# A two-layer vision tower on one core: weights centred before x lands, means accumulated beside, and one-hot products, first sums and gate products reordered

## What is computed

```
h = patches @ Wp + bp + (relu(xy @ W1 + b1) @ W2 + b2)      # embedding and position
h = h + attn0(LN(h))        # 8 query heads of 64, one shared key and value
h = h + ffn0(LN(h))         # gelu MLP, only for the tokens whose weight ranks in the top 31 of an image
h = h + attn1(LN(h))        # bias per key from the LAST edge that points at it, out of 16384 edges
h = h + moe(LN(h))          # top 2 of 8 experts
```

## Time and profile before

| what | value |
|---|---|
| median of three timed runs | 71.36 us |
| the profiled execution, its own time | 71.47 us |
| its span, first to last instruction | 69.6 us |
| PE matmul busy | 60.6 us, 87% of the span |
| DVE / ACT / POOL busy | 41.7 / 29.7 / 13.5 us |
| share of the chain that ended last | PE 61%, DVE 12%, DMA 9%, ACT 7%, POOL 3% |

### The profile page before, as it was taken

One profiled execution on the slowest core, in us unless ns is written; L12 is line 12 of the kernel. 1 busy time (PEld: TensorE's weight loads), 2 busy tenths in 40 slices (PEclk: granted clock), 3 DMA queues, 4 the chain that ended last, 5 costly groups with the idle time before them and its releaser, 6 DMA issues.

```text
span 69.6 us, 1990 instructions
## 1 busy us (share of the span) xinstructions
PE 60.6 (87%) x830; PEld 39.6 (57%) x839; DVE 41.7 (60%) x111; ACT 29.7 (43%) x69; POOL 13.5 (19%) x32
## 2 busy tenths in 40 slices
PE   3995896999999999999989995959999969989940
PEld 1330462787698578564448565548794318654910
DVE  2491039975699995535962546999563025756830
ACT  0240012431748852177764425259604283953030
POOL 6800039200000892058304000000000004000000
PEclk9999999999999999999999999999999999999999
DMA  0799999950000000000000000000000000000003
GB/s 0 182 381 370 392 225 243 235 175 0 0 9 0 0 0 9 0 0 5 0 0 0 0 9 5 0 9 0 0 9 0 0 0 0 0 0 0 0 0 75
DMA packets 2390, 4.07 MB, mean 58 GB/s; under 512 B 780, under 2 KB 1230, under 8 KB 2382
## 3 DMA queue, kind: packets, MB, share of 16 engines
q1 hardware_dynamic: 1568, 3.49, 17.4%
q10 hardware_dynamic: 781, 0.46, 2.2%
q0 software_dynamic: 32, 0.00, 0.0%
HBM read 3.82 MB, written 0.13 MB: 57 GB/s over the span
## 4 chain that ended last, share of the span: by engine, by line
PE 61%; DVE 12%; DMA 9%; ACT 7%; POOL 3%; issue 3%; DVEq 0%; ACTq 0%; POOLq 0%
DMA Xt<-in_x_dram 9%; PE psum L717 8%; PE psum L711 6%; DVE top L533 4%; ACT ge L457 3%; POOL WoS L300 3%; PE psum L727 3%; PE psum L928 3%; PE psum L974 3%; PE psum L819 3%; PE psum L770 3%; PE psum L1066 2%; PE psum L746 2%; DVE E L632 2%; DVE top L630 2%
## 5 line engine op out<-in xcount | busy, mean ns | idle before, releaser
L717 PE MATMUL psum<-warm 128*128 128x512 bf16 x44 | 14.5, 441 | 1.7 <-DVE warm L479 1.2
L717 PEld LDWEIGHTS psum<-warm 128*128 128x128 bf16 x53 | 5.2, 109 | 6.8 <-issue 3.6
L300 POOL TENSOR_TENSOR WoS<-pack_attn,top 128x256 f32<-128x256 f32 x5 | 3.1, 647 | 10.1 <-DVE top L540 10.1
L492 DVE TENSOR_TENSOR onehot<-idb,iota 128x2048 bf16<-128x2048 bf16 x4 | 4.8, 1241 | 0.0
L335 POOL TENSOR_TENSOR resT<-hT,xC 128x256 f32<-128x256 f32 x1 | 0.7, 724 | 20.0 <-DVE xC L661 20.0
L428 ACT ACTIVATE E<-E 128x512 f32<-128x512 f32 x4 | 2.5, 631 | 3.1 <-DVE E L632 3.1
L727 PE MATMUL psum<-Xt,pack_wp 128*64 128x256 f32 x16 | 2.2, 390 | 1.1 <-DMA Xt<-in_x_dram 1.1
L457 ACT ACTIVATE ge<-psum,pack_moe 128x512 f32<-128x512 f32 x4 | 2.5, 687 | 1.2 <-PE psum L1026 1.2
L711 PE MATMUL psum<-pack_ident,E 128*128 128x128 f32 x16 | 2.5, 276 | 0.7 <-DVE E L632 0.7
L630 DVE TENSOR_REDUCE top<-psum 128x8 f32<-128x512 f32 x4 | 2.7, 683 | 0.4 <-PE psum L943 0.4
L498 DVE TENSOR_TENSOR centre<-pack_ident,mean 128x128 f32<-128x128 f32 x1 | 0.3, 293 | 4.4 <-DMA pack_ident<-in_ident_dram 4.4
(11 more groups left out here) (206 smaller groups left out, 134.6 us busy)
## 6 DMA issues: line engine op xcount, KB each, us to landing
Xt<-in_x_dram SPq DMA_DIRECT2D x1, 1024.0 KB, 6.4
Xt<-in_x_dram SPq DMA_DIRECT2D x1, 512.0 KB, 7.4
pack_both<-in_both_dram SPq DMA_DIRECT2D x2, 240.2 KB, 8.8
pack_moe<-in_moe_dram SPq DMA_DIRECT2D x1, 450.0 KB, 9.8
pack_mid<-in_mid_dram SPq DMA_DIRECT2D x1, 327.5 KB, 9.7
pack_attn<-in_attn_dram SPq DMA_DIRECT2D x1, 288.0 KB, 8.0
pack_expert<-in_expert_dram SPq DMA_DIRECT2D x2, 130.0 KB, 9.4
pack_wp<-in_wp_dram ACTq DMA_DIRECT2D x1, 192.0 KB, 5.8
```

The lines of the kernel that those rows point to most:

```text
L300: gp.tensor_tensor(WoS[:, s, 4 * u:4 * u + 4, :].rearrange("p (b n) d -> p b n d", b=2), bc(WoT[:, 2 * u:2 * u + 2, :], 1, 2), bc(top0[:, ...
L492: ve.tensor_tensor(onehot[:, 16 * k:16 * k + 16, :], bc(idb[:, k, :], 1, 16), iota16[:, :, :], ALU.is_equal).then_inc(s_hot, 1)
L717: mm(B[bank][:, :], lhsT=warm[:, 0:P], rhs=warm[:, :], start=True, stop=True)
```

## The change

1. **Centred weights.** Since the centring is linear, DVE subtracts each weight row's own mean from it (`centred`: a sum over 64 columns, then one multiply-add) for pos, for k-blocks 0 and 1, and for 2 to 5. The embedding products then give the centred h directly in B[1]; the copy ACT L378 and the product L751 ahead of the square go, `hT[0]` is copied after the square.
2. **Loads.** On ACT's queue pos goes before wp, and wp becomes two loads (128 rows of 512 bytes, 128 rows of 1 KB). ident stays last, now behind two loads of 128 rows and one of 66.
3. **Token means apart.** The mean that was left out is rebuilt in B[3]: `token_mean(q)` (a pair of 64 x 256 float32 matmuls per k-block), six of them, and the position's mean (L902 after). They stand mostly where `keep_clock` calls stood; ACT copies the result (`meanT`), POOL adds it (`hM`) before the last residual.
4. **Order.** The position products come first. `last_rows(0)` goes between the embedding's k-blocks 3 and 4; half of the head products goes after the variance product. Several fillers go.
5. **First softmax.** The exponentials, sum and reciprocal of slot 0 run as two halves of 4 heads; POOL makes `WoS[1]` whole (6 pieces in place of 5), ACT takes half of slot 2, DVE half of slot 3 alone.
6. **Later.** The rank product goes ahead of the second half of L895; `attrT` is copied by ACT, after its table load, instead of DVE; L911 goes ahead of L909. The K products use one more bank, and DVE waits for them one at a time.

```diff
+            act.dma_start(pack["wp"][:, 0:2 * D], packs["wp"][:, 0:2 * D]).then_inc(in_wp, 16)
+            act.dma_start(pack["wp"][:, 2 * D:], packs["wp"][:, 2 * D:]).then_inc(in_wpr, 16)
...
+            def centred(dst, src, sums, n):
+                ve.tensor_reduce(sums, src, X, ALU.add).then_inc(s_wsum, 1)
+                dve.wait_ge(s_wsum, n)
+                ve.scalar_tensor_tensor(dst, bc(sums, len(src.shape) - 1, D), -1.0 / D, src, ALU.mult, ALU.add).then_inc(s_wpc, 1)
+
+            dve.wait_ge(in_pos, 16)
+            centred(posc[:, :].unsqueeze(1), posW2.unsqueeze(1), wsum[0:D + 2, KX:KX + 1], 1)
+            dve.wait_ge(in_wp, 16)
+            centred(Wpc[:, 0:2, :], Wp[:, 0:2, :], wsum[:, 0:2], 2)
             hot(0)
+            dve.wait_ge(in_wpr, 16)
+            centred(Wpc[:, 2:KX, :], Wp[:, 2:KX, :], wsum[:, 2:KX], 3)
+            hot(1)
...
+            def token_mean(q):
+
+                pe.wait_ge(s_wmean, 1)
+                for c in range(2):
+                    ins = mm(B[3][rows[c], 0:HALF], lhsT=wmean[:, q:q + 1].broadcast_to([P, D]), rhs=Xt[:, c, q, :],
+                             start=False, stop=(q == KX - 1), skip_group_check=True)
+                return ins
...
-            keep_clock(5, 2)
-            for k in range(2):
+            token_mean(3)
+            def ffn_out(k):
+
                 pe.wait_ge(s_gelu, k + 1)
...
+            ffn_out(0)
             pe.wait_ge(const_l1, 1)
             pe.wait_ge(s_cmp, 1)
+            pe.wait_ge(s_gelu, 2)
...
+            ffn_out(1).then_inc(s_y, 1)
             pe.wait_ge(s_res, 1)
             for h, cols in enumerate(HALVES):
                 mm(B[HCS[2][h]][:, cols], lhsT=centre[:, :], rhs=resT[:, cols], start=True, stop=False)
+            pe.wait_ge(s_attrT_ev, 1)
+            mm(B[7][0:TOK, D:D + HEADS], lhsT=attrT[:, :], rhs=WeB, start=True, stop=True).then_inc(s_eb, 1)
```

More of the change, by code:

```diff
@@ L392, in _ @@
             act.wait_ge(s_shift, 1)
-            for i in range(HEADS):
-                ins = sc.activation(E0[:, 0, i, :], B[i // 4][:, i % 4 * TOK:(i % 4 + 1) * TOK], ACT.Exp,
-                                    bias=shift[:, i:i + 1], scale=SC0)
-            ins.then_inc(s_exp0, 1)
+            for u in range(2):
+                for i in range(4 * u, 4 * u + 4):
+                    ins = sc.activation(E0[:, 0, i, :], B[i // 4][:, i % 4 * TOK:(i % 4 + 1) * TOK], ACT.Exp,
+                                        bias=shift[:, i:i + 1], scale=SC0)
+                ins.then_inc(s_exp0h, 1)
             for s in range(1, SLOTS):
@@ L747, in last_rows, with head_products @@
                 ins.then_inc(s_expo, 1)
-            pe.wait_ge(s_centre, 1)
-            pe.wait_ge(s_h, 1)
-            mm(B[1][:, 0:HALF], lhsT=centre[:, :], rhs=hT[0][:, :], start=True, stop=True).then_inc(s_hc, 1)
-            pe.wait_ge(in_attn0, 16)
-            for k in range(4):
+            def head_products(k):
                 for c in range(2):
@@ L756, in _ @@
                     ins = mm(B[5][rows[c], k * D:(k + 1) * D], lhsT=Wq0[D:P, k, :], rhs=Wk0[D:P, :], start=True, stop=True)
-            ins.then_inc(s_g, 1)
+                return ins
+            def token_mean(q):
[3 more added lines that the diff above has]
+                             start=False, stop=(q == KX - 1), skip_group_check=True)
+                return ins
+            pe.wait_ge(in_pos, 16)
+            mm(B[4][0:D, 0:P], lhsT=posW1, rhs=grid, start=True, stop=True).then_inc(s_posh, 1)
+            keep_clock(3, 1)
+            pe.wait_ge(s_wpc, 1)
+            pe.wait_ge(s_posh_ev, 1)
+            pe.wait_ge(s_warm, 2)
+            for c in range(2):
+                mm(B[1][rows[c], 0:HALF], lhsT=posc[:, :], rhs=bc(posh[:, :], 1, 2), start=True, stop=False)
+            keep_clock(3, 2)
+            pe.wait_ge(s_wpc, 2)
+            pe.wait_ge(in_x[0], 16)
+            embed(0)
+            embed(1)
+            pe.wait_ge(s_wpc, 3)
+            embed(2)
+            embed(3)
+            last_rows(0)
+            pe.wait_ge(in_x[1], 16)
+            embed(4)
+            embed(5).then_inc(s_hc, 1)
+            pe.wait_ge(in_attn0, 16)
+            head_products(0)
+            head_products(1)
+            pe.wait_ge(s_blk, 3)
             pe.wait_ge(s_sq, 1)
             mm(B[2][:, 0:HALF], lhsT=mean64[:, :], rhs=sq[0][:, :], start=True, stop=True).then_inc(s_var, 1)
-            keep_clock(3, 2)
-            for k in range(4):
+            head_products(2)
+            head_products(3).then_inc(s_g, 1)
+            for k in range(1, 4):
                 last_rows(k)
-            keep_clock(3, 2)
             pe.wait_ge(s_x, 1)
@@ L844, in _ @@
             shift0(3)
+            pe.wait_ge(s_exp0h, 2)
+            keep_clock(0, 1)
+            mix0(0)
             pe.wait_ge(s_exp0, 1)
-            keep_clock(0, 3)
-            mix0(0)
-            pe.wait_ge(s_exp0, 2)
-            keep_clock(2, 1)
+            pe.wait_ge(s_wmean, 2)
+            for c in range(2):
+                mm(B[3][rows[c], 0:HALF], lhsT=wmean[0:D + 2, KX:KX + 1].broadcast_to([D + 2, D]), rhs=bc(posh[:, :], 1, 2),
+                   start=True, stop=False, skip_group_check=True)
             mix0(1)
@@ L857, in _ @@
             pe.wait_ge(s_key, 1)
-            tr(B[3][0:TOK, 0:P], last[:, 0, :], P).then_inc(s_keyT, 1)
-            keep_clock(4, 2)
+            tr(B[2][0:TOK, 0:P], last[:, 0, :], P).then_inc(s_keyT, 1)
+            token_mean(0)
+            pe.wait_ge(s_centre, 1)
             pe.wait_ge(s_h, 2)
@@ L920, in _ @@
             ins.then_inc(s_kb, 1)
-            keep_clock(4, 4)
+            token_mean(4)
+            token_mean(5).then_inc(s_hm, 1)
             pe.wait_ge(s_x, 5)
```

157 lines of the change are left out of this document (81 added, 76 removed).

## The result

The change made the kernel **slower**: 73.12 us, the median of four executions (72.68 to 73.46), against 71.40 (71.33 to 71.47) for the kernel before on the same chip. The ratio is 1.022, 95% interval 1.017 to 1.027. I had forecast 71.2, with a range up to 72.0. The profiled execution took 72.68 with a span of 70.9, against 71.47 and 69.6 before: 1.2 us to explain, and some 0.4 in the median that this one execution does not show. (Ratios here leave out executions more than 1.5% above the fastest of the same kernel; medians hold them all.)

A forecast was written before the change was run, and what follows sets the result against it. No engine's total work was the limit, but which input of key instructions came last at four places. The terms -0.45 + 0.1 + 0.45 - 0.25 gave -0.15, so 71.2 us against the median 71.36, range 70.6 to 72.0.

The forecast's parts named there:

- Term A: The start up to the first queries: they come at 15.45 instead of 15.90, -0.45 us.
- no wait: Embedding: row_pow is ready at 10.9, before PE reaches last_rows(0) at 11.15, so PE does not wait.
- `ident` at 10.5: Loads at the start: ident lands at 10.5, chosen between 9.88 by bytes and 11.6 by rows.
- Rival 4: Loads served by rows, so they land later: start +0.35, sum +0.65, 72.0 us; chance 0.12.
- The cast at 0.31: Start: row_pow is ready 0.31 behind ident, as in the kernel before.
- Rival 5: PE's clock falls in new idle holes near 7.5, 9.1 and 11.2: 72.5 us; chance 0.08.
- Term B: First softmax: mix0(1) must now wait for POOL's fourth piece, +0.1 us.
- Term C: Second layernorm: token_mean(1) ahead of L925 delays bo_col, xC[1] and the token weights, +0.45 us.
- Term D: Feed-forward to K products: yG comes earlier, but its product waits behind attrT's edge-bias product; -0.25 us.
- the -0.45 that I had named for D without the wait: Feed-forward to K products: the gain if the attrT wait were absent, -0.45 us.
- "slower": Outcome for the whole kernel: the change makes it slower; chance 0.35, against faster 0.45 and same 0.20.

The follow-up runs named there:

- z2: y1 with the embedding weights wp loaded in one piece again: 73.29 us, ratio 1.024.
- w1: z2 without the five fillers ahead of the one-hot products: 72.01 us, ratio 1.004.
- z4: The kernel before with only the softmax part of the change: 71.60 us, ratio 0.998.
- x3: The changed kernel with ident loaded ahead of the second piece of wp: 78.11 us.
- x4: The changed kernel with token_mean(1) moved behind the products of bo_col: 73.26 us.
- y3: The changed kernel with the first one-hot group behind the whole embedding, four more fillers before the embedding, and token_mean(1) behind the bias rows: median 71.91 us.
- y4: The changed kernel with row_pow copied by ACT, four more fillers before the embedding and one before the first one-hot products: 72.20 us, ratio 1.010.
- w3: w1 with DVE's first one-hot piece, hot(0), moved behind the second centring: 72.75 us.
- y1: The changed kernel with nine fillers where PE idled in the embedding, five of them ahead of the first one-hot products: 72.99 us, ratio 1.020.
- w2: v1 with token_mean(0) moved from ahead of hT's centring into the wait for sq, one filler taking its old place: 71.64 us, ratio 1.000.
- z3: y1 with the edge-bias product put behind the yG products: 72.93 us.
- v1: y3 with row_pow copied by ACT, first one-hot group in PE's wait for sq, fillers around the other three, edge-bias product behind yG products: 71.20 us, ratio 0.9935.

## Why the prediction was wrong

**Term A: -0.45 forecast, +1.12 measured. The wrong step** is the one that said that `last_rows(0)` finds `row_pow` at 10.9 and has "no wait": it waited 1.32. The steps up to there were near: rest of `wp` landed at 9.07 (9.1 chosen), first piece at 7.60 (7.2), the eight passes at 1.08. So were the steps behind it: `xC` starts 2.38 behind the centred sum (2.35 forecast). Of the 1.57 between the queries forecast (15.45) and measured (17.02), 1.46 lie at the first one-hot product, 12.61 instead of 11.15. Two numbers made the wait.

*`ident` at 10.5.* I had 9.88 by bytes and 11.6 by rows, and took a value between. It landed at 11.23 in this profile and at 11.2 to 12.2 in all with the split. Rival 4, "the queue is served by rows", to which I had given 0.12, was right on `ident`, and even its own 11.6 was not the late end; its other landings (first piece at 8.1, the weights ready at 10.9) did not come (7.60, 10.15). z2 and w1 show the cause: one load less, `ident` at 9.2, and without the fillers 1.0 to 1.1 us of time back.

I had also started from a late point. The load's sixteen shares land one by one, and the last one counts: in the kernel before they had their median at 8.41 and the last at 9.85, in z4, with the same loads, 8.50 and 8.70; in the changed kernel 10.55 and 11.23. By the median share the split moved `ident` by 2.1. Some 0.5 us of it may be the issue, which ACT reaches at 2.80 instead of 2.3 behind one load more (w1); the rest passes between issue and landing, 8.4 us instead of 6.9.

The Trainium skill's rule that I had quoted ("DMA: Bandwidth & Descriptors", "Queues, rings and completion order": turns between queues, by the packet) would make more and smaller rows late at equal bytes; the landings agree in sign, but no run shows the turns themselves (the queue carried 925 packets instead of 781), and 128 rows more cost more (2 to 3 us against w1) than the 1.7 that I had worked out by rows.

*The cast at 0.31.* It took 1.19. I took a duration from the earlier trace rows without asking what it contained. That row starts at 9.90 beside DVE's `centre` (9.88, 0.29 us) and ends 0.04 behind it. In all thirteen profiles with this cast on GpSimd it ended 0.04 to 0.05 behind the DVE instruction that was running when it began, whatever was left of that: from 0.24 in x3 over 0.40 in x4, 0.69 in w1 and 0.85 in y3 to 1.19 in the changed kernel. On ACT, 0.20 to 0.21 beside the same DVE work. The Trainium skill ("SBUF — State Buffer", "Who interferes with whom") says that a DVE instruction with two SBUF inputs contends with a GpSimd instruction that reads SBUF, over a shared port pair that works as an exclusive lock; the trace agrees, 1.19 against 1.22 of the one-hot piece. y4 shows what a short copy is worth: 0.8, of which 0.2 in its profile were `ident`'s earlier landing. I had moved the cast, by `ident`'s landing, under 1.22 us pieces that stand back to back.

The two overlap: once `ident` is early (w1) the cast's 0.69 is hidden, once the cast is short (y4) 0.7 is gone, with `ident` still late. An estimate from the rows of the changed kernel: with `ident` at 10.5 the cast would have ended behind the one-hot piece of 10.07, near 11.3, and cost some 0.2; with the landing of 11.23 and 0.31 for the cast the wait would have been some 0.4; together it was 1.32. With both out of the way and `hot(0)` moved (w3) the queries come at 15.45. Rival 5, the clock, is not the cause of the median (y1, 72.99 at a full clock in all four executions). It may be part of the scatter: two of the changed kernel's four executions have a mean clock of 0.97, but the slowest, 73.46, has 1.00. What the 0.4 between this profile and the median are stays open.

**Term B: +0.1 forecast, -0.28 measured** (z4: about -0.2), a wrong sign. The mechanism, `mix0(1)` behind POOL's fourth piece (24.85 + 1.20, then 26.09), was right. Mis-sized was POOL's start: I let half a sum bring it 0.3 earlier. The reduction fell from 0.69 to 0.41 and could begin while ACT worked on the second four heads; POOL began at 23.53, 0.49 earlier when the lag of 1.12 is taken off.

**Term C: +0.45 forecast, +0.66 measured.** The wait was the one named: `bo_col` idle 1.66 for PE's L929 instead of 1.01, and x4 took 0.39 of it away. Mis-sized was the pair: I had taken 0.48 from a pair of another shape (30.50 to 30.98), and `token_mean(1)` holds PE from 31.42 to 32.01, 0.59. With the variance products 0.92 late (30.78 against 29.86) and the token weights 1.50, the stretch between them costs 0.58, which is this pair. The other 0.08 arises ahead of it. In the kernel before:

```profile
28.46 0.49 DVE L566 TENSOR_TENSOR hT<-hT,psum 128x128 f32<-128x128 f32 x2 [1.28 <-PE psum L831]
...
29.00 0.71 PE L862 MATMUL psum<-hT,centre 128*128 128x128 f32 x4
...
29.86 0.71 PE L866 MATMUL psum<-sq,mean 128*128 128x128 f32 x4
```

The centring products came 0.54 behind the add there and 0.63 in the changed kernel. `token_mean(0)`, which stands ahead of them now, is the obvious suspect, but w2 has it elsewhere and still shows 0.63; so these 0.08 stay open, and costing that pair at nothing was not the mistake.

**Term D: -0.25 forecast, -0.18 measured at the K products and -0.24 at `qT`**, by the mechanism named. The gate's product starts 1.44 behind the kernel before (37.99 against 36.55), 0.06 less than the token weights' 1.50, as forecast (0.05); the variance product 1.22 (38.84 against 37.62), so that 0.28 was gained there and 0.10 lost again by the K products. `attrT`'s copy starts as the table load ends (37.48), PE's edge product follows at 37.78 and `yG`'s at 37.99. z3 and v1 take that wait away and give 0.19 in their profiles; the -0.45 that I had named for D without the wait does not follow from my own 0.5 and 0.2, which make -0.7, but -0.18 or -0.24 with another 0.19 comes near it.

**The sum** would have been +1.26 with these sizes (D at `qT`); three of the four terms carried their mechanism, though B with the wrong sign, and the one that failed was the largest. I had given "slower" 0.35.

## What to carry to other kernels

Splitting or reordering a load can move the loads behind it on its queue, and not by bytes (here 9.2 to 11.2 and later): when a later one feeds the critical path, read its slack first, and take the late bound, not the middle. Before a duration is carried to another place, look at what ran beside it: a GpSimd instruction that reads SBUF may be short only because DVE's neighbour was (the same cast took 0.24 to 1.19). A product put ahead of others that are waited for costs its own length (`token_mean(1)`, 0.59), and the length is taken from its own shape. And a filler that holds the clock can itself hold the path: z2 hid a gain of 1 us behind five of them.
